# The last attention layer: each score matmul beside a peak matmul in TensorE's row halves, instead of two scores and then two peaks

## What is computed

```
qkv = (x @ W_qkv + b_qkv)                       # 4 heads of 8 channels, n = 1024 tokens per image
scores = einsum('bhnd,bhmd->bhnm', q, k) / sqrt(32)
out = einsum('bhnm,bhmd->bhnd', softmax(scores), v) @ W_proj + b_proj
t = t + out
router_probs = softmax(ln(t) @ router_w + router_b);  top 2 of 8 experts, weights normalised
t = t + sum of the two experts' answers, by their weights
```

## Time and profile before

| | us |
|---|---|
| median of 3 runs | 6140.09 |
| lowest, highest | 6136.86, 6146.87 |
| the profiled execution, its own time | 6144.6 |
| its span, first to last instruction | 6142.8 |
| mean granted TensorE clock in it, share of full speed | 0.961 |

### The profile page before, as it was taken

The page is one execution under the profiler, slowest core; times in us unless marked ns, Lnnn a source line. Parts: engine busy times, 40 slices in busy tenths (PEclk is TensorE's granted clock), DMA queues, the critical chain, the costliest instruction groups (busy, mean ns, idle before and its releaser), DMA issues.

```text
span 6142.8 us, 145812 instructions
## 1 busy us (share of the span) xinstructions
PE 5357.5 (87%) x43064; PEld 2193.0 (36%) x43064; DVE 4961.8 (81%) x9311; ACT 4802.8 (78%) x8146; POOL 3144.7 (51%) x3711
## 2 busy tenths in 40 slices
PE   6679999999999998468999899999999899989997
PEld 5234444444444444442222222222222222222222
DVE  7857767676676675749999899999999899989995
ACT  1159989899898998216888888888888888888887
POOL 1147777777777776622444444443444444434443
PEclk9889999999999999778999999999999999999999
DMA  3010000000000000230000000000000000000000
GB/s 114 23 46 10 10 9 10 11 10 9 11 10 9 10 10 7 67 110 7 9 9 9 10 9 9 8 9 9 9 9 9 10 9 9 9 10 9 9 8 5
DMA packets 400110, 104.64 MB, mean 17 GB/s; under 512 B 348546, under 2 KB 398675, under 8 KB 398803
## 3 DMA queue, kind: packets, MB, share of 16 engines
q1 hardware_dynamic: 398163, 94.72, 7.1%
q10 hardware_dynamic: 1152, 0.05, 0.0%
HBM read 61.17 MB, written 33.56 MB: 15 GB/s over the span
## 4 chain that ended last, share of the span: by engine, by line
PE 24%; DVE 16%; issue 8%; ACT 3%; POOL 3%; DVEq 1%; ACTq 0%; POOLq 0%
DVE d_peaks L2352 13%; PE d_p_o L2195 7%; PE d_p_s L2182 5%; PE d_p_k L2211 5%; ACT d_wt L2077 2%; PE d_p_s L2284 2%; POOL d_rstd L1989 2%; PE d_p_s L2168 2%; PE d_p_s L2242 1%; PE d_p_s L2233 1%; DVE d_total L2362 1%; POOL d_xl L1993 1%; ACT d_answers L2073 1%; DVE d_rank L2444 1%; DVEq L2347 1%
## 5 line engine op out<-in xcount | busy, mean ns | idle before, releaser
L2352 DVE TENSOR_REDUCE d_peaks<-d_p_k 128x1 f32<-128x512 f32 x4096 | 2612.6, 685 | 241.6 <-PE d_p_k L2211 220.3
L2077 ACT ACTIVATE d_wt<-d_p_s 128x512 f32<-128x512 f32 x4096 | 2200.8, 617 | 413.9 <-PE d_p_s L2182 413.3
L830 ACT ACTIVATE b_wt<-b_sq 128x1024 f32<-128x1024 f32 (+3 forms) x1536 | 1240.2, 845 | 8.4 <-issue 8.4
L2195 PE MATMUL d_p_o<-d_wt,d_v_pad 128*32 128x512 f32 x8192 | 1095.1, 607 | 2.5 <-ACT d_o_sb L2082 1.9
L2211 PE MATMUL d_p_k<-d_kT,d_qT 64*128 64x512 bf16 x4096 | 801.6, 386 | 207.3 <-DVE d_peaks L2352 186.0
L739 POOL TENSOR_TENSOR b_sq<-b_sq 128x1024 f32<-128x1024 f32 (+1 forms) x512 | 849.5, 1680 | 231.4 <-DVE b_sq L1037 231.4
L819 ACT ACTIVATE b_sq<-b_p_s 128x1024 f32<-128x1024 f32 (+2 forms) x1024 | 775.5, 757 | 186.7 <-PE b_p_s L890 180.5
L2182 PE MATMUL d_p_s<-d_qT,d_kT 64*128 64x512 bf16 x4096 | 801.8, 387 | 60.5 <-ACT d_wt L2077 40.5
L1037 DVE TENSOR_TENSOR b_sq<-b_p_s,bc_tri 128x1024 f32<-128x1024 f32 (+1 forms) x512 | 551.8, 1089 | 268.5 <-PE b_p_s L890 208.3
L2032 POOL TENSOR_TENSOR d_answers<-d_answers,d_mix 128x2048 f32<-128x2048 f32 x64 | 233.0, 3640 | 955.9 <-DVE d_mix L2453 955.9
L903 PE MATMUL b_p_o<-b_wt,b_v_pad 128*32 128x512 f32 (+2 forms) x6144 | 676.5, 513 | 2.0 <-ACT b_wt L830 1.0
(11 more groups left out here) (293 smaller groups left out, 7532.9 us busy)
## 6 DMA issues: line engine op xcount, KB each, us to landing
c_slots<-t SPq DMA_DIRECT2D x128, 128.0 KB, 2.5
a_xt<-in_x SPq DMA_DIRECT2D x4, 2048.0 KB, 14.8
a_w<-in_L_conv_W SPq DMA_DIRECT2D x64, 128.0 KB, 2.8
t<-a_rows SPq DMA_DIRECT2D x32, 256.0 KB, 2.4
b_x_in<-t SPq DMA_DIRECT2D x64, 128.0 KB, 2.7
t<-b_result SPq DMA_DIRECT2D x64, 128.0 KB, 2.2
t<-c_slots SPq DMA_DIRECT2D x64, 128.0 KB, 1.9
d_x_in<-t SPq DMA_DIRECT2D x64, 128.0 KB, 2.7
```

The lines of the kernel that those rows point to most:

```text
L830: act.activation(wt[:, n % RING, :, 0:m], sq[:, n % SQ_RING, :, 0:m], ACT.Silu, scale=1.0 / D).then_inc(weighed, 1)
L2077: act.activation(wt[:, n % RING, :], tile(n)[:, :], ACT.Exp, scale=SCALE).then_inc(s_used, 1)
L2195: ins = pe.matmul(p_o[32 * h:32 * h + 32, :], v_pad[:, slot, kb, h, :], wt[:, (H * a + h) % RING, :], start=(kb == 0), stop=(kb == J - 1), ...
L2352: dve.tensor_reduce(peaks[:, m, r:r + 1], bank((m, r))[:, :], X, ALU.max).then_inc(k_used, 1)
```

## The change

Two scores and two peaks that stood as score, score, peak, peak become score (rows 0 to 63), peak (rows 64 to 127), peak (rows 0 to 63), score (rows 64 to 127). For that the peak of the odd head comes first in its pair, on PE, in the bank ring and on DVE. Each matmul waits for its own bank alone; the two waits for the second of a pair are gone. The first four matmuls of a window keep score, score, peak, peak (the odd peak first), since the peaks there follow a wait for the window before.

```diff
 def k_order(on):
...
-        out += [(2 * a, 0), (2 * a, 1)] if "next" in on else []
+        out += [(2 * a, 1), (2 * a, 0)] if "next" in on else []
...
-                def scores(n):
+                def score(n):
                     qc, kb, h = UNITS[n]
-                    wait(pe, s_used, win.s_done(n + 1) - S_BANKS)
-                    for r in range(2):
-                        rows = slice(64 * r, 64 * r + 64)
-                        pe.matmul(seat(n + r)[:, :], kT[rows, win.slot("own"), h // 2, kb * P:(kb + 1) * P],
+                    rows = slice(64 * (h % 2), 64 * (h % 2) + 64)
+                    pe.matmul(seat(n)[:, :], kT[rows, win.slot("own"), h // 2, kb * P:(kb + 1) * P],
...
-                def peak(m):
+                def peak(m, r):
                     j, g, half = PEAKS[m]
-                    if m == 0:
-                        arrived(s_used, win.settled)
-                    slot = win.slot("next")
-                    wait(pe, k_used, win.k_done((m, 1)) - K_BANKS)
-                    for r in range(2):
...
+                def scores_and_peaks(n, m):
+
+                    if "own" in win.on:
+                        score(n)
+                    if m == 0:
+                        if "own" in win.on:
+                            score(n + 1)
+                        if "next" in win.on:
+                            arrived(s_used, win.settled)
+                    if "next" in win.on:
+                        peak(m, 1)
+                        peak(m, 0)
+                    if "own" in win.on and m:
+                        score(n + 1)
...
                 for a in range(GROUPS):
-                    if "own" in win.on:
-                        scores(H * a)
-                    if "next" in win.on:
-                        peak(2 * a)
+                    scores_and_peaks(H * a, 2 * a)
                     for name in misc(K_MISC, a, win.on) + misc(S_MISC, a, win.on):
                         use_misc(name)
-                    if "own" in win.on:
-                        scores(H * a + 2)
-                    if "next" in win.on:
-                        peak(2 * a + 1)
+                    scores_and_peaks(H * a + 2, 2 * a + 1)
...
                 def peak(m):
-                    for r in range(2):
+                    for r in (1, 0):
                         dve.tensor_reduce(peaks[:, m, r:r + 1], bank((m, r))[:, :], X, ALU.max).then_inc(k_used, 1)
```

More of the change, by code:

```diff
@@ L1684, in k_order @@
     for a in range(GROUPS):
-        out += [(2 * a, 0), (2 * a, 1)] if "next" in on else []
+        out += [(2 * a, 1), (2 * a, 0)] if "next" in on else []
         out += misc(K_MISC, a, on)
-        out += [(2 * a + 1, 0), (2 * a + 1, 1)] if "next" in on else []
+        out += [(2 * a + 1, 1), (2 * a + 1, 0)] if "next" in on else []
     return out
@@ L2175, in seat @@
                     return p_s[win.s[name][1]]
-                def scores(n):
+                def score(n):
                     qc, kb, h = UNITS[n]
-                    wait(pe, s_used, win.s_done(n + 1) - S_BANKS)
-                    for r in range(2):
-                        rows = slice(64 * r, 64 * r + 64)
-                        pe.matmul(seat(n + r)[:, :], kT[rows, win.slot("own"), h // 2, kb * P:(kb + 1) * P],
-                                  qT[rows, win.slot("own"), h // 2, qc * HALF:(qc + 1) * HALF],
-                                  start=True, stop=True).then_inc(s_made, 1)
+                    rows = slice(64 * (h % 2), 64 * (h % 2) + 64)
+                    pe.matmul(seat(n)[:, :], kT[rows, win.slot("own"), h // 2, kb * P:(kb + 1) * P],
+                              qT[rows, win.slot("own"), h // 2, qc * HALF:(qc + 1) * HALF],
+                              start=True, stop=True).then_inc(s_made, 1)
                 def add_up(i, slot, a):
@@ L2201, in free_bank @@
                     return p_k[win.k[name][1]]
-                def peak(m):
+                def peak(m, r):
                     j, g, half = PEAKS[m]
-                    if m == 0:
-                        arrived(s_used, win.settled)
-                    slot = win.slot("next")
-                    wait(pe, k_used, win.k_done((m, 1)) - K_BANKS)
-                    for r in range(2):
-                        rows = slice(64 * r, 64 * r + 64)
-                        pe.matmul(free_bank((m, r))[:, :], qT[rows, slot, g, j * P:(j + 1) * P],
-                                  kT[rows, slot, g, half * HALF:(half + 1) * HALF], start=True, stop=True).then_inc(k_made, 1)
+                    slot = win.slot("next")
+                    rows = slice(64 * r, 64 * r + 64)
+                    pe.matmul(free_bank((m, r))[:, :], qT[rows, slot, g, j * P:(j + 1) * P],
+                              kT[rows, slot, g, half * HALF:(half + 1) * HALF], start=True, stop=True).then_inc(k_made, 1)
+                def scores_and_peaks(n, m):
+                    if "own" in win.on:
+                        score(n)
+                    if m == 0:
+                        if "own" in win.on:
[7 more added lines that the diff above has]
+                        score(n + 1)
                 def turn_o(i, half):
@@ L2500, in body @@
                     if "next" in win.on and m == PAIRS // 2:
-                        dve.wait_ge(k_used, win.k_done((PAIRS // 2 - 1, 1)))
+                        dve.wait_ge(k_used, win.k_done((PAIRS // 2 - 1, 0)))
                         shift_most(nx, 0)
```

## The result

The changed kernel takes 6068.57 us, median of 4 (6057.7 to 6073.09), against 6138.48, median of 4, for the kernel before: ratio 0.9879, 95% interval 0.9868 to 0.9891, 1.2% faster. Forecast were 6071 and a range of 6020 to 6130. The size came true. Where it comes from did not, in good part: that is what the experiments show.

A forecast was written before the change was run, and what follows sets the result against it. No single engine bounds the window; the chain of waits passes among DVE, PE and ACT. Gains of 0.67 + 0.22 + 0.23 = 1.12 us a window, times 62 windows, 69.4 us, gave 6071 us; range 6020 to 6130.

The forecast's parts named there:

- Group 3: Odd pair's scores stand for ACT's second Exp; score and peak would go ahead, PE gaining 0.45 us a window.
- Group 4, DVE another 0.22: Peak after the first projection starts with the score, 0.22 us earlier; with group 3's 0.45, DVE gains 0.67 us.
- Groups 7 to 10: PE carries the chain at unchanged length; at its end the peak starts with the score: 0.22 us a window.
- Groups 14 and 15: Window's end: peaks earlier by 0.09 in group 14 and 0.14 in 15, 0.23 us, inherited by the next window's peaks.
- The registers for the waits: Register instructions for PE's waits: as many as before, less the shared ones; cost taken as zero.
- DVE is the bound: nothing: Stretches where DVE carries the chain, such as group 10 to group 13, were forecast to gain nothing.
- The second score 0.22 later: Each pair's second score comes 0.22 us later or more, covered by ACT's first Exp; uncovered, 0.22 per pair.
- A: Only the peaks' earlier slot counts, group 3's early start fails: 0.44 us a window, 6113 us; chance 0.18.
- D: More of DVE's waits lie on the chain than one window shows: 1.66 us a window, 6037 us; chance 0.10.
- B: Mates don't run side by side, as PE's sequencer passes waits singly: 0.14 us per last score, 6139 us; chance 0.10.
- C: Last score held behind peaks starves ACT: up to 2.6 us a window, 6178 us at two thirds; chance 0.07.
- the signs named: Add_up at 1.9 us in group 3, window 50.6 to 50.7, PE busy falling, DVE's peak waits about 120 in all.

The follow-up runs named there:

- the scores' old wait alone: New order, with the old wait for the second score's bank put back ahead of the first score; peaks wait for their own banks: 6100.18 us, 0.9926 of the kernel before.
- The seven pairs: Kernel before, with new order and own waits only in the odd pairs of groups 3, 4, 10 and both pairs of 14, 15: 6114.57 us, ratio 0.9950.
- Own waits alone: Kernel before with its matmul order kept in every pair, but each matmul waiting for its own bank alone: 6102.88 us, ratio 0.9928.
- The doubled waits: Old order with own waits, the own wait of each pair's second matmul written twice: 6153.97 us, ratio 1.0016 to the kernel before.
- the dead waits: Changed kernel plus two waits, long over, in every pair but the first, ahead of first score and first peak: 6084.04 us, 0.9898 of the kernel before.
- the doubled ones in the new order: Changed kernel with the own waits of each pair's second peak and last score written twice: 6165.5 us, ratio 1.0033 to the kernel before.
- for the peaks alone: New order, with the old wait for the second peak's bank put back ahead of the first peak; scores wait for their own: 6143.13 us, 0.9999 of the kernel before.

## Why the prediction was right, and where it was not

**The sum.** 1.12 us a window were forecast, 1.09 came, and 62 of them make 67.6 us. In the profiled executions the layer gained 76.7: of the rest 4.8 came at the turns of the loop and about 4 elsewhere in the layer, unforecast. The stretches with the three terms of the sum gave 0.65 for 1.12 (0.30 in groups 3 and 4, 0.13 in 9 and 10, 0.22 in 13 to 15); 0.43 came from groups 0 to 2 and 5 to 8, which stood at nothing. So the right total is in good part luck, two errors that met: one price too high and one left at zero.

**Group 3, forecast 0.45; too high.** The mechanism was right: the scores' old wait alone puts 0.40 back into groups 3 and 4. But the 0.37 between scores and peaks was not the rule. In the median window before, the peaks follow the scores of that pair by 0.22 and add_up starts 2.18 after the first score, not 2.34; now 1.88. That is 0.30, and the whole of groups 3 and 4 gained 0.30. I took a size from one window.

**Group 4, DVE another 0.22.** It came, but as a shift and not as a vanished wait: measured from the group's first score, the first maximum comes 0.18 earlier (0.46 for 0.64) in groups 3, 4, 10, 14 and 15, and the `residual` and the wait of 0.39 behind it came along. Up to group 4's end the window had gained 0.59, forecast 0.67: of it 0.29 before group 3.

**Groups 7 to 10, forecast 0.22.** 0.13 in groups 9 and 10; of the 0.14 of groups 5 to 8, 0.10 hangs on the peaks' own waits, as shown above.

**Groups 14 and 15, forecast 0.23.** 0.22 in groups 13 to 15, up to the next window's first maximum. From first score to first score groups 14 and 15 last 2.62 and 2.64, where it was 2.78, so 0.30 less, but group 0 behind them lasts 2.90 for 2.79. The condition I named, that the next window's peaks inherit it, held only in part: the head waits 0.45. The seven pairs lost all of it there.

**The registers for the waits, costed at zero: the step that failed.** I counted the instructions and not which of them carries the wait. Own waits alone are worth 0.64 of the 1.09. Part of that is the form: a standing register op puts the load 0.112 behind the semaphore, a wait on the load itself 0.042 to 0.058; group 14 gains its 0.08 that way. Part is that the first matmul of a pair no longer stands for the bank of the second; groups 5 to 8 gain by that at the places shown above. How the whole 0.64 divides stays open. The doubled waits do not settle it: they take back 0.78, more than all of it, since they bring the slow form back and put an instruction between mates, which the kernel before did not have. "DVE is the bound: nothing" was wrong because the loop was DVE, PE's answer, DVE, and the answer came late.

**The second score 0.22 later, costed at zero.** Held with own waits. In group 1 the second Exp follows the first by 0.76 where it was 0.49, and in group 2 by 0.69; the groups 0 to 2 are faster all the same.

**The rivals.** A (6113) and D (6037): by time neither, though A's doubt of group 3 was just. B: in the changed kernel mates start together where their banks are free, so it did not happen; but its mechanism is real and its price was too low: 0.14 a last score there, 0.19 measured in group 14 of the doubled waits. With an instruction more between the mates the order gains nothing, 6165.5 us. C: ACT's idle for scores fell from 6.2 to 4.9 in the window, so it did not happen. The Trainium skill's rule that matmuls start and end in program order (TensorE: Matmul & The Clock Gate, "The mechanism") agrees with the traces here, by starts: of the changed kernel's last scores, 1736 looked at, none starts before its second peak. Its delay found cover in the changed kernel.

**Of the signs named**, add_up in group 3 (1.88) and the window (50.65) came as said. PE's busy time did not fall but rose, 5357.5 to 5411.5: two peaks that start 0.22 apart cover 0.60, where two that start together covered 0.39. The wait of DVE for peaks fell to 167.9, not to 120, and in the window to 2.3, not to 1.5. The waits of 0.25 did not vanish either: in groups 3 and 4 they are 0.23 and 0.40, as the maxima ahead of them moved too, in 14 and 15 they halved, and the one at the head, which was to stay, grew to 0.45.

## What to carry to other kernels

In a queue that runs matmuls in pairs, let each matmul wait for its own bank alone, and let the wait ride on that matmul. Here this was worth 0.64 us a window, more than the reordering on top of it (0.45). A wait for more than that, written between two mates, splits their slot: 1.10 us in a window of 51. An instruction of its own between mates costs whether its wait stands or not. Waits long over, on register ops that are there anyway and are passed well ahead, were free in the window. So look in the trace for the instruction that carries each wait and for when it is reached. After an order is changed, look for the next point that stands for something else, since gains ahead of it are lost until it is freed.

## What the runs showed of the hardware that I had not expected

From the rise of a semaphore to the weight load that stood for it: 0.042 us for a peak and 0.058 for a score where the load itself carries the wait, 0.112 where a register op ahead of it does (0.028, then 0.084), 0.105 where an event semaphore instruction does (0.028, then 0.077). With such an instruction between them, mates that could start together start 0.19 apart in group 14.

The turn of the loop costs. Over the four turns the windows around them exceed the usual distance by 19.7 us before, 14.9 in the changed kernel, 29.7 with the dead waits and 33.8 with the doubled ones in the new order. So the dead waits, free in a window, were not free at the turn: 29.7 less 14.9 is about the difference between their median and the changed kernel's. The price does not follow the number of PE's instructions. The doubled waits in the old order have as many as those in the new (577 and 575 records in a window) and exceed by only 20; the old waits for the scores alone and for the peaks alone have the same number (513) and exceed by 14.5 and 19.9. What it follows is open.
